# Expert rows turned by a transposing DMA, and a new order of VectorE's work in attention

## The reference, cut to what matters

```python
# attention layer, per batch
h      = layernorm(x)                               # 1024 x 1024
q, k   = ctx @ Wq.T + bq, ctx @ Wk.T + bk           # 1024 x 128 each
att    = softmax(q @ k.T)                           # 1024 x 1024
x      = x + einsum('bln,bmn->blm', h, att)
# expert layer, over all 4096 tokens
h      = layernorm(x)
logits = h @ gate_w.T + gate_b                      # 32 experts
top 4 experts of each token, weights = softmax of their 4 logits
for each expert e, for the rows of h sent to it:
    g   = min(h @ w_gate[e] + b_gate[e], 7)         # 1024 -> 512
    u   = clip(h @ w_up[e] + b_up[e], -7, 7)
    out = ((u + 1) * g * sigmoid(1.702 * g)) @ w_down[e] + b_down[e]    # 512 -> 1024
x      = x + weighted sum of each token's 4 outs
```

## Time and profile before

| | |
|---|---|
| median of three runs | 3115.03 us |
| the profiled execution | 3116.04 us |
| its span, first to last instruction | 3113.9 us |
| PE busy | 95% of the span |
| DVE, ACT, POOL busy | 55%, 38%, 18% |
| mean granted TensorE clock | 0.984 of 2.4 GHz |
| attention and routing | 0 to about 715 us |
| expert tiles | about 720 to 3095 us |

### The profile page before, as it was taken

The page is one execution under the profiler, slowest core; times in us unless marked ns, Lnnn a source line. Parts: engine busy times, 40 slices in busy tenths (PEclk is TensorE's granted clock), DMA queues, the critical chain, the costliest instruction groups (busy, mean ns, idle before and its releaser), DMA issues.

```text
span 3113.9 us, 44999 instructions
## 1 busy us (share of the span) xinstructions
PE 2948.7 (95%) x14948; PEld 1512.9 (49%) x14949; DVE 1716.4 (55%) x2856; ACT 1178.8 (38%) x1235; POOL 563.5 (18%) x502
## 2 busy tenths in 40 slices
PE   6798988987999999999999999999999999999997
PEld 2354545553544455544445444454445444445443
DVE  3687878674454544555544555555555544553532
ACT  2332323233343433444433434444343433442422
POOL 1032322331111111111111111111111111111111
PEclk8899999988999999999999999999999999999999
DMA  6776656556554655755655756575565555565333
GB/s 192 175 182 176 176 151 174 181 159 207 158 162 101 178 140 144 220 162 159 191 141 143 224 148 195 162 227 151 151 200 155 162 157 160 155 178 139 75 66 61
DMA packets 343541, 501.38 MB, mean 161 GB/s; under 512 B 190881, under 2 KB 190881, under 8 KB 343234
## 3 DMA queue, kind: packets, MB, share of 16 engines
q0 software_dynamic: 45856, 152.33, 22.2%
q10 hardware_dynamic: 94576, 225.46, 20.4%
q1 hardware_dynamic: 203058, 122.94, 15.0%
HBM read 354.64 MB, written 112.46 MB: 150 GB/s over the span
## 4 chain that ended last, share of the span: by engine, by line
PE 75%; DVE 1%; ACT 0%; issue 0%; DMA 0%; ACTq 0%; POOL 0%; SPq 0%; POOLq 0%
PE psY L1291 24%; PE psG L1269 21%; PE psU L1269 21%; PE psX L1275 4%; PE psG L1327 3%; PE psA L1282 2%; DVE gt L1219 0%; ACT aT L1134 0%; DVE gt L1222 0%; DMA acc<-y,idxs 0%; DMA idxs<-slots 0%; ACT xT L1130 0%; ACTq L1056 0%; POOL acc L1121 0%; ACTq L1028 0%
## 5 line engine op out<-in xcount | busy, mean ns | idle before, releaser
L1291 PE MATMUL psY<-W,aT 128*128 128x512 f16 x3456 | 769.6, 379 | 23.5 <-ACT aT L1134 23.5
L1269 PE MATMUL psG<-W,xT 128*128 128x512 f16 x3072 | 686.5, 380 | 4.3 <-ACT xT L1130 4.3
L1269 PE MATMUL psU<-W,xT 128*128 128x512 f16 x3072 | 683.9, 379 | 0.0
L1291 PEld LDWEIGHTS psY<-W,aT 128*128 128x128 f16 x3456 | 336.9, 98 | 402.7 <-ACT aT L1134 27.5
L1269 PEld LDWEIGHTS psG<-W,xT 128*128 128x128 f16 x3072 | 300.5, 98 | 369.7 <-issue 9.1
L1269 PEld LDWEIGHTS psU<-W,xT 128*128 128x128 f16 x3072 | 300.6, 98 | 333.9
L1097 POOL DMA_INDIRECT acc<-y,idxs x143 | 225.3, 1575 | 1051.0 <-DVE y L1210 1008.0
L1210 DVE SCALAR_TENSOR_TENSOR y<-bias,idxs,y 128x1024 f32<-128x1024 f32 x143 | 183.7, 1285 | 389.3 <-ACT y L1141 389.3
L653 PE MATMUL psM<-W,XT 128*128 128x512 f16 x1392 | 355.9, 379 | 8.6 <-DVE xr L900 8.6
L1092 POOL DMA_INDIRECT xg<-xn_tab,idxg x145 | 156.8, 1082 | 953.1 <-PE psX L1275 902.8
L1141 ACT ACTIVATE y<-psY,idxs 128x1024 f32<-128x1024 f32 x143 | 159.2, 1114 | 438.1 <-DMA idxs<-slots 406.8
(11 more groups left out here) (157 smaller groups left out, 2634.3 us busy)
## 6 DMA issues: line engine op xcount, KB each, us to landing
stage_more<-in_L_ffn_w_down ACTq DMA_DIRECT2D x62, 1024.0 KB, 10.0
stage<-in_L_ffn_w_gate ACTq DMA_DIRECT2D x60, 1024.0 KB, 6.7
stage_more<-in_L_ffn_w_up ACTq DMA_DIRECT2D x31, 1024.0 KB, 5.6
stage<-in_L_ffn_w_up ACTq DMA_DIRECT2D x30, 1024.0 KB, 12.4
stage<-in_x SPq DMA_DIRECT2D x32, 512.0 KB, 5.4
xr<-in_x SPq DMA_DIRECT2D x32, 512.0 KB, 4.7
acc<-xr SPq DMA_DIRECT2D x32, 512.0 KB, 3.8
xn_tab<-x2h SPq DMA_DIRECT2D x32, 512.0 KB, 3.0
```

Source lines behind the costliest of these rows:

```text
L1269: op = pe.matmul(ps[:], xT[:, k, :, a], weights(par, c, offset + k * I, I), start=k == 0 and n == 0, stop=k == KH - 1 and n == 2)
L1291: op = pe.matmul(psY[:, h * HALF:(h + 1) * HALF], aT[:, k, :, a], weights(par, c, 2 * KH * I + k * H + h * HALF, HALF), start=k == 0 and n ...
```

## The change

**Experts.** `xn_tab` rows become all HI/LO halves one after the other (x2h is [2, H], LO row then HI row, instead of interleaved pairs). In an expert's first step PE still transposes the rows of the next tile, now as 16 float16 blocks of 128 x 128. In every other step SP issues one transposing DMA from `xg` into a new buffer `xT_next`, after waiting for ACT's copy of the tile before (`s_xTev`); ACT copies `xT_next` to `xT` after the up matmuls. The half step loses its transposes. ACT evacuates psA before the sigmoid.

**Attention.** DVE computes the second layernorm's statistics where it did, but normalises in the next step behind the maximum (`second_norm`); softmax scale goes before the first normalisation; in alone steps the LO parts of tile s-1 come behind the maximum of tile s, and the exponential, which overwrites `prob`, waits for them. The four one-hot rows become one instruction, the four reductions become a multiply and a reduction, and `wt` is gone. PE's transposes of `xs2` move from matmul 10 to 16, the logits from 2 to 4. Queries and keys of the second batch are computed quarter by quarter in alone steps 4 to 7, in psM, psQ and psR; those of later batches start in psE. At the start Wq and Wk are transposed in one go, ctx is loaded before the small constants, the first ctx pairs use three PSUM tiles, and gate_w is transposed after the queries and keys.

```diff
-        x2h = sb("x2h", [P, 2, H, 2], F16)
+        x2h = sb("x2h", [P, 2, 2, H], F16)
...
+        def quarter(bk, n):
+            if batch(bk) == 0:
+                return (psM_halves + psE_halves)[n]
+            return early[n] if batch(bk) == 1 else (psE_halves + psM_halves)[n]
...
             sp.dma_start(wqk_in[:, 1, :], g["Wk"]).then_inc(s_wqk, 16)
+            load_ctx(0)
...
                 def exponent():
                     act.wait_ge(s_nmx, tile(b1, s + 1))
+                    act.wait_ge(s_alo, tile(b1, s))
...
+            for n in range(2 * KC):
+                op = pe.transpose(psT[:, n * D:(n + 1) * D], wqk_in[:, n // KC, n % KC * P:(n % KC + 1) * P], ident[:])
+            op.then_inc(s_wT, 1)
...
                 for n in range(4):
+                    if n == 0 and not first(bk):
+                        pe.wait_ge(s_exp, NT * batch(bk))
+                    if n == 2 and not first(bk):
+                        pe.wait_ge(s_x2, NT * (batch(bk) - 1))
+                    one_quarter(bk, n)
...
-                held = range(10, 10 + KH)
+                held = range(16, 16 + KH)
...
+                    if s in QK_ALONE:
+                        n = QK_ORDER[s - QK_ALONE[0]]
+                        pe.wait_ge(s_cTev, per(NT // 2, following(b1), NT // 4 * (n % 2 + 1)))
+                        one_quarter(following(b1), n)
...
+            def second_norm(bt, n):
+                if n >= 1 or batch(bt) > 0:
+                    alone(dve, s_x2T, tile(bt, n), s_past)
+                normalise(1, xs2[:], xr[:, n % 2, :], s_xs2, tile(bt, n))
...
+                    if b2 is None and s > 0:
+                        lo_parts(s - 1)
+                    if b2 is not None and s > 0:
+                        second_norm(*late)
                     dve.wait_ge(s_x1[s % 2], per(8 * NT, b1, 16 * (s // 2 + 1)))
-                    layernorm(0, xs[:], x1[:, s % 2, :], s_xs, tile(b1, s))
+                    statistics(0, x1[:, s % 2, :], tile(b1, s))
...
+                    link(v, dve.tensor_tensor(junk[:, :, :], oh[:, j], every_k(rk), ALU.mult))
+                    v.inc(dve.tensor_reduce(dest_f[:], junk[:, :, :], AX_X, ALU.add))
...
+                    link(v, dve.tensor_tensor(oh[:, j], every_k(iota_e),
+                                              i4[:, :].rearrange("p (k o) -> p k o", o=1).to_broadcast([P, TOPK, E]), ALU.is_equal))
...
                 load_slots(sp, idxg, i + 2, s_idxg)
+                if turn:
+                    alone(sp, s_xTev, i + 1, s_past)
+                    sp.dma_start_transpose(out=xT_next[:, :, :, :].rearrange("p a k q -> p (a k) q"), in_=xg[:, :]).then_inc(s_X, 16)
...
             with pool.Fori(1, last) as j:
-                pool.wait_ge(s_X, j + 3)
+                pool.wait_ge(s_X, 16 * j + 48)
                 gather(j + 3)
...
+            def evac_x(i, turned):
+                act.wait_ge(s_X, 16 * i + 16)
+                if turned:
+                    act.wait_ge(s_U, i)
+                src = xT_next[:].rearrange("p a k q -> p (a k q)") if turned else psX[:]
+                act.activation(xT[:].rearrange("p a k q -> p (a k q)").bitcast(F32), src.bitcast(F32), ACT.Copy).then_inc(s_xTev, 1)
...
+                guarded(act, prev_guard, lambda: evac_a(i - 1))
                 act.wait_ge(s_gmin, i + 1)
                 act.activation(sg[:], gt[:], ACT.Sigmoid, scale=ALPHA).then_inc(s_sig, 1)
-                guarded(act, prev_guard, lambda: evac_a(i - 1))
...
-                for n in range(KH):
-                    op = pe.transpose(psX[:, n * P:(n + 1) * P], xg_w[:, n * P:(n + 1) * P], ident[:])
-                op.then_inc(s_X, 1)
+                for n in range(2 * KH):
+                    op = pe.transpose(psX[:, n * P:(n + 1) * P], xg[:, n * P:(n + 1) * P], ident16[:])
+                op.then_inc(s_X, 16)
...
-                pe.wait_ge(s_xg, 16 * i + 32)
-                transpose_rows()
+                if not turned:
+                    pe.wait_ge(s_xg, 16 * i + 32)
+                    transpose_rows()
...
-                pe.wait_ge(s_xg, 16 * i + 32)
-                transpose_rows()
                 down(i - 1, par)
...
-                    step(t0, e, par, True, pair > 0 if par == 0 else None)
-                    with pe.Fori(t0 + 1, tf) as i:
-                        step(i, e, par, False, None)
+                    step(t0, e, par, True, pair > 0 if par == 0 else None, False)
+                    step(t0 + 1, e, par, False, None, True)
+                    with pe.Fori(t0 + 2, tf) as i:
+                        step(i, e, par, False, None, True)
```

More of the change, by code:

```diff
@@ L539, in step @@
                     act.wait_ge(s_xs2, tile(bt, n + 1))
-                    act.activation(x2h[:, n % 2, :, HI], xs2[:], ACT.Copy, scale=S_ROWS).then_inc(s_hi2, 1)
+                    act.activation(x2h[:, n % 2, HI, :], xs2[:], ACT.Copy, scale=S_ROWS).then_inc(s_hi2, 1)
                     act.wait_ge(s_x2T, tile(bt, n + 1))
@@ L902, in step @@
                     alone(dve, s_x2, tile(b2, s + 1), s_past)
-                    if late:
-                        alone(dve, s_x2T, tile(b2, s), s_past)
-                    layernorm(1, xs2[:], xr[:, s % 2, :], s_xs2, tile(b2, s))
+                    statistics(1, xr[:, s % 2, :], tile(b2, s))
+                    if b1 is None or s == NT - 1 or own is False:
+                        second_norm(b2, s)
                     if b1 is None and s >= 3:
@@ L1080, in _ @@
                     t0, t1 = start_of(sp, e), start_of(sp, e + 1)
-                    step(t0, pair > 0 if par == 0 else None)
-                    with sp.Fori(t0 + 1, t1) as i:
-                        step(i, None)
+                    for j in range(len(CUT)):
+                        step(t0 + j, pair > 0 if par == 0 and j == 0 else None, j > 0)
+                    with sp.Fori(t0 + len(CUT), t1) as i:
+                        step(i, None, True)
             tt = start_of(sp, E)
```

192 lines of the change are left out of this document (96 added, 96 removed).

## The result

The changed kernel took 3400.37 us (median of 4 runs, 3391.16 to 3405.51) against 3115.53 us before (4 runs, 3114.66 to 3118.11): ratio 1.0909, interval 1.0883 to 1.0936. The forecast was 2950 us, its range 2912 to 3015. It is 285 us slower than before, and outside the range.

What follows compares the result with a forecast made beforehand. PE was taken to bound the expert part, DVE attention's steps of both. Expert part -97 + 4 - 23 + 10 = -106 us and attention -60 us gave -166, from 3113.9 to a forecast of 2950 us, range 2912 to 3015.

Steps and rivals of the forecast that it cites:

- Row transposes leave PE: Expert part: 112 of 145 transpose sets leave PE at 0.87 us each, all on the path, -97 us.
- psA before the sigmoid: Expert half tiles: psY no longer waits for aT, -23 us, bounds -25 and 0.
- fp16 blocks: Expert part: the 33 sets staying on PE become 16 float16 blocks, taken at 1.0 us a set, +4 us.
- Attention, -60 us: Attention: -40 in steps of both, -6.5 second batch's queries and keys, -7 alone steps, -6.5 start.
- the first maximum: Attention's start: fewer ctx waits, earlier ctx, moved gate_w transposes, less low clock; -6.5 us, bounds -3 and -10.
- the alone steps: Attention's alone steps: 8.52 us each falls to 7.6, -7 us over 8 steps, bounds 0 and -12.
- the queries and keys of the second batch: Attention, change to second batch: 22.4 us between maxima falls to 15.9, -6.5 us, bounds 0 and -8.
- the steps of both: Attention's steps of both: shorter DVE pace, 15.75 us, and earlier batch starts, together -40 us, bounds -48 and -15.
- I take 10 us of waits in all, bounds 0 and 96 us: Expert part: waits for transposes late behind weight loads, +10 us; upper bound is 3 us in one tile per expert.
- 3 to 6 us late: Expert part: lateness of gather and transpose in the tile after a 3 MB load, against 2 to 6 us slack.
- Rival (b): Expert part: weight loads make one tile per expert late, the 96 us bound, 3036 us; chance 0.12.
- Rival (d): Expert part: transpose and gather loop through xg takes 18.4 us in every tile, 3233 us; chance 0.05.

Runs made afterwards that it cites:

- e1: Changed kernel with TensorE transposing every tile's rows again, nothing turned by DMA; attention's new order and psA before the sigmoid kept: 3033.45 us.
- e2: Changed kernel with weight loads from the third expert on cut to 32 KB instead of 1 MB (stale weights, other output): 2927.94 us.
- e5: e1 with psA's evacuation put back behind the sigmoid, as in the kernel before: 3056.24 us.
- m1: Measurement by itself: a 512 KB transposing DMA beside weight loads, 11 settings; landed in 4.3 us alone, 11.4 behind 3 MB.
- m2: Measurement by itself: scatter and bias broadcast added beside the transpose, 10 settings; 3 MB of loads 11.4 us, with both 18.6.
- m3: Measurement by itself: timing and kind of scatter beside the transpose, 10 settings; 1.5 MB of loads 8.1 us, with scatter 12.5 to 13.1.
- e10: Changed kernel with each weight load of experts 2 and on halved to 512 KB (half of those weights stale): 3695.28 us.
- e12: e10 with POOL holding each tile's scatter until the transpose in flight has landed: 3280.01 us.
- e11: Changed kernel with POOL holding each tile's scatter until the transpose in flight has landed, full loads: 3419.99 us.

## Why the prediction was wrong

By its own steps:

- **Row transposes leave PE, -97 us: right.** From e1 to e2 the time falls by 105.5 us. psX cost PE 0.87 us in the earlier trace rows; 112 sets of fp16 blocks at 0.89 us (1.0 was taken) are 100 us, and PE's waits in front of psG are another 4 us shorter in e2. The 0.89 us lie between these two starts in the changed kernel:

```profile
1036.00 1.06 PE L1321 MATMUL psX<-ident,xg 128*128 128x128 f16 x16
1036.89 0.38 PE L1337 MATMUL psY<-W,aT 128*128 128x512 f16 x1
```

- **psA before the sigmoid, -23 us: right,** 22.8 us (e5 against e1). psY waited 1.3 us for aT in the changed kernel, 23.5 before.
- **Attention, -60 us: right in kind, 6 us too cautious.** In the trace the first row transposes start 66.5 us earlier (648.45 against 714.94): 8.6 us are won up to the first maximum (6.5 was taken), 12.0 in the alone steps (7), 6.4 at the queries and keys of the second batch (6.5) and the rest, 39.5, in the steps of both (40). That e5 is 59.6 us below the kernel before, almost the forecast, is luck: its expert part is 7 us longer, some 3 of them from 145 sets of fp16 blocks at 0.89 us, 2 from longer waits of psY for aT (25.8 us against 23.5); the last 2 are open. A step of both takes 15.84 us (15.75 was worked out, 17.5 before), an alone step 6.9 to 7.2 (7.6 was taken), as the starts of L938 and of the maximum L862 show; from the last alone maximum, at 85.22, to the next batch's, at 101.27, are 16.05 us (15.9 was worked out, 22.4 before).

```profile
159.35 1.22 DVE L938 SCALAR_TENSOR_TENSOR xr<-psM,xr 128x1024 f32<-128x1024 f32 x1
175.19 1.22 DVE L938 SCALAR_TENSOR_TENSOR xr<-psM,xr 128x1024 f32<-128x1024 f32 x1
```

```profile
50.22 1.22 DVE L862 TENSOR_REDUCE mx<-psE 128x1 f32<-128x1024 f32 x1
57.15 1.23 DVE L862 TENSOR_REDUCE mx<-psE 128x1 f32<-128x1024 f32 x1
```

- **"I take 10 us of waits in all, bounds 0 and 96 us": this step failed.** It came to 472 us. The three measured parts, 59.6, 22.8 and 105.5, lead from 3115.5 to 2927.6. Without its 10 us of waits the forecast is 2940, so the rest of the sum was 12 us too cautious, and this term alone turned the sign.

Why it failed: the transposes beside the loads were priced by a share. The share said 0.86 with loads and 3 to 4 us for a transpose, hence "3 to 6 us late". But a transpose issued behind 3 MB isn't slowed by a share: by itself it then took 11.4 us (m1), 7 more than alone, and what is issued beside it, scatter and biases, comes on top, to 18.6 (m2). The bytes issued just ahead should have been counted, and when: ACT issues the loads at the end of a tile's step, SP the transpose 0.8 us behind. An estimate from the rows of before: 3 MB at the 331 GB/s that the prediction itself worked out are 9.5 us, and 5.7 + 9.5 = 15.2 us for a transpose, 15.2 + 4.5 + 1.06 + 0.7 = 21.5 us for the loop. That is 5.5 us past the tile's 16, twice for each of 30 experts: some 330 us, more than the 176 that the rest of the sum wins. Measured were 25.0 and 28.1 us. So the sign could be had from the rows of before, though m1's 11.4 shows that this way of adding isn't exact.

The rows also held the hint: 7642 ns of issue beside a 2 MB load. Rival (b) quoted it and set against it that gathers in the same bursts never took over 6.8 us. That comparison misled: behind 3 MB a gather goes from 3.9 to 7.5 us, a transpose of as many bytes from 4.3 to 11.4.

Rival (b) had the place right (a tile behind each burst) and the price wrong, 3 us for one tile instead of 8 us (472 / 60) for each of two. Rival (d) had the mechanism (transpose, gather and index load in one loop through one `xg`) but spread it over every tile; ACT didn't wait for 52 of the 112 transposes. Neither priced what follows a wait on PE, over 100 us at the lower clock.

For (d) the prediction also weighed the Trainium skill ("VectorE: DVE Perf Modes", The three transpose paths), from whose 1309 ns a block comes the estimate of 20.9 us a tile. Alone a tile takes 4.3 us in these runs, so that figure isn't what made the loop too long. A rule that was not weighed bears on it: the Trainium skill ("Trainium Kernel Development and Optimization", Key Constraints) states that DMAs issued from different engines' queues all run on the same 16 DMA engines and interleave. The trace agrees, 4.3 us against 11.4 behind another queue's 3 MB.

**What stays open.** In m3 a transpose behind 1.5 MB with a scatter took 13.1 us, in e10 20.1, more than the 18.3 in the changed kernel behind 3 MB. Holding the scatter brings e10's median between 1000 and 1300 us from 19.6 down to 9.0, so it needs the two together as far as e12 shows, but why it is worst with small loads no run shows. Why 1 MB of biases weighs more than 1 MB of weights wasn't tried either. Nor was it tried to give `xg` a second buffer, which would take the gather out of the loop.

## What to carry to other kernels

Before work moves from a busy engine to a DMA, list what is issued in the microseconds ahead of it on every queue, and count those bytes into its landing; a mean share of the DMA engines says nothing on that. If it meets a burst, issue the burst behind the DMA that has a deadline (once its issue has ended is enough, its own queue isn't needed; beginning together, as in e11, isn't), and check that nothing small which the next stage needs stands behind the burst or behind something that the burst slows. Where a DMA and a gather take turns on one buffer, the next of them starts late by the whole delay, burst after burst.

## What the runs showed of the hardware, not expected

- Beside loads a scatter delays a transpose by more than its bytes' share: 4.3 us alone, 8.1 behind 1.5 MB of loads, 12.5 to 13.1 with a 0.5 MB scatter more; the same tile as an ordinary copy 2.9 alone, 7.6 with both.
- 1 MB of broadcast biases delays a transpose to 11.9 us, 1 MB of weights to 7.1.
- An issue can block the queue: 1.8 us alone, 7.3 behind 3 MB, up to 17.4 in the changed kernel; behind loads in its own queue 9.6.
- DMA engines can be busy at 0.82 to 1.2 by their packets' time and move 39 to 142 GB/s (e10); a busy share isn't a rate.
- Halving the bytes of a burst made the kernel slower, 3400 to 3695 us; with the scatter held as well it took 3280.
